# A routed two-FFN block on one core: the sync engine's list work moved two steps behind each list, and the closing sums shared by two engines

## The reference

```python
x = x + 0.5 * ffn(layernorm(x))     # 8 experts of width 256, the best 2 of them per token
x = x + attention(layernorm(x))     # 16 heads of 4, on the first 64 columns
x = x + 0.5 * ffn(layernorm(x))     # the same experts again

def ffn(xt):
    logits = xt @ gate_w.T + gate_b
    top_v, top_i = top_k(logits, 2)
    act = (xt @ w0.T + b0) * silu(xt @ w1.T + b1)          # per expert
    out_all = act @ w2.T + b2
    return sum over the 2 chosen of softmax(top_v) * out_all[chosen]
```

## Time and profile before

| | us |
|---|---|
| median of 3 runs | 752.5 (751.33 to 753.72) |
| the profiled execution, time | 752.53 |
| its span, first to last instruction | 750.8 |
| PE busy | 579.4 (77%) |
| DVE busy | 435.4 (58%) |
| POOL busy | 372.7 (50%) |
| ACT busy | 349.5 (47%) |

### The profile page before, as it was taken

One profiled execution on the slowest core, in us unless ns is written; L12 is line 12 of the kernel. 1 busy time (PEld: TensorE's weight loads), 2 busy tenths in 40 slices (PEclk: granted clock), 3 DMA queues, 4 the chain that ended last, 5 costly groups with the idle time before them and its releaser, 6 DMA issues. The chain is left out here.

```text
span 750.8 us, 14409 instructions
## 1 busy us (share of the span) xinstructions
PE 579.4 (77%) x4460; PEld 437.2 (58%) x4460; DVE 435.4 (58%) x1627; ACT 349.5 (47%) x806; POOL 372.7 (50%) x415
## 2 busy tenths in 40 slices
PE   3428995999971167988888888889898699699960
PEld 2317885889960023555555555556554489598950
DVE  6664461223332277678888888888863464244436
ACT  2004542455530002666666666666677356365530
POOL 4877750000007887445476767553422467566650
PEclk9999998999995555899999999999999799899985
DMA  8547653554611111111122222111100355555529
GB/s 281 166 124 248 192 188 119 195 163 149 198 43 39 51 55 49 50 49 49 49 63 63 63 63 62 56 50 49 59 21 16 118 168 189 173 171 170 172 66 332
DMA packets 65026, 86.01 MB, mean 115 GB/s; under 512 B 11096, under 2 KB 46648, under 8 KB 64152
## 3 DMA queue, kind: packets, MB, share of 16 engines
q1 hardware_dynamic: 52184, 63.29, 26.3%
q0 software_dynamic: 8640, 17.97, 7.8%
q10 hardware_dynamic: 4128, 3.83, 1.5%
HBM read 31.85 MB, written 30.56 MB: 83 GB/s over the span
## 5 line engine op out<-in xcount | busy, mean ns | idle before, releaser
L1164 DVE TENSOR_REDUCE attn_nm<-ps 128x2 f32<-128x512 f32 x256 | 168.9, 684 | 61.5 <-PE ps L883 59.8
L987 ACT ACTIVATE attn_pt<-ps 128x512 f32<-128x512 f32 x256 | 146.4, 594 | 74.4 <-PE ps L867 71.7
L671 DVE SCALAR_TENSOR_TENSOR experts_act<-ps,route_cols,experts_silu 128x256 f32<-128x256 f32 x170 | 81.4, 483 | 165.7 <-ACT experts_silu L635 165.5
L603 PE MATMUL ps<-experts_xT,experts_w 128*128 128x256 f32 x680 | 170.0, 394 | 0.0
L379 POOL DMA_INDIRECT x_rows<-route_xn,route_rows x128 | 125.3, 979 | 52.7 <-issue 34.8
L883 PE MATMUL ps<-attn_ka,attn_qa 128*128 128x256 bf16 x512 | 106.5, 295 | 47.7 <-DMA attn_qa<-kq_pieces 29.4
L603 PEld LDWEIGHTS ps<-experts_xT,experts_w 128*128 128x128 f32 x680 | 126.4, 196 | 15.0
L635 ACT ACTIVATE experts_silu<-ps,route_cols 128x256 f32<-128x256 f32 x170 | 80.2, 473 | 75.2 <-PE ps L603 74.7
L614 PE MATMUL ps<-w_table,experts_act 128*128 x680 | 101.5, 286 | 1.6 <-ACT experts_y_tokens L652 0.9
L867 PE MATMUL ps<-attn_qa,attn_ka 128*128 128x256 bf16 x512 | 99.3, 278 | 4.4 <-ACT attn_pt L987 2.4
L707 POOL DMA_INDIRECT y_tokens<-experts_y_tokens,experts_to x78 | 75.4, 966 | 43.4 <-ACT experts_y_tokens L652 28.5
(11 more groups left out here) (163 smaller groups left out, 712.9 us busy)
## 6 DMA issues: line engine op xcount, KB each, us to landing
experts_w<-w_table SPq DMA_DIRECT2D x85, 256.0 KB, 2.5
experts_x<-x_rows SPq DMA_DIRECT2D x85, 132.0 KB
y_rows<-experts_y_tokens SPq DMA_DIRECT2D x46, 128.0 KB, 1.9
x_rows<-no_rows SPq DMA_DIRECT2D x24, 132.0 KB
kq_pieces<-attn_kqp SPq DMA_DIRECT2D x16, 192.0 KB
x_rows<-route_xn,route_rows POOLq DMA_INDIRECT x128, 2.8
second_y<-y_tokens SPq DMA_DIRECT2D x8, 256.0 KB, 7.0
second_y<-y_tokens ACTq DMA_DIRECT2D x8, 256.0 KB, 7.4
```

What stands on the lines that cost most here:

```text
L603: mm = pe.matmul(ps[:, q % 2 * 2 + k, w * SLOTS:(w + 1) * SLOTS], m["w"][:, q % WR, at + k * P:at + (k + 1) * P], m["xT"][:, q % 2], start ...
L671: nc.vector.scalar_tensor_tensor(out=m["act"][:, q % 2, k], in0=ps[:, q % 2 * 2 + k, SLOTS:2 * SLOTS], scalar=route["col"](part, at, CH + ...
L987: nc.scalar.activation(pt[:, g % 2, j, :], ps[:, SBK[h % 2], :], ACT.Exp, scale=SCALE).then_inc(exp_done, 1)
L1164: nc.vector.tensor_reduce(nm[:, qc, 2 * pair:2 * pair + 2], ps[:, SA[k], :].rearrange("p (j t) -> p j t", t=S), AX.X, ALU.max, negate=True ...
```

## The change

SP's list work is split. `sp_list` keeps the blank rows, the wait for the list and the register loads; it is called two steps behind DVE's list, at step 13 for part 1 and at step 52 for part 3 (ahead of the loop for part 0, and where it was for part 2). A new `sp_rows`, at the part's first block, keeps the waits for sent rows and blank rows. At the end the sums are made 512 columns (two batches) at once: DVE takes six of the eight pairs, POOL takes pairs 2 and 5, and a semaphore counts each pair of loads.

```diff
     def sp_list(sp, part):
-        region = REGION_OF[part]
         if closed(part):
             for at in route["tails_of"](sp, part):
-                sp.dma_start(rows_of(x_rows[region % 2], at), const["no_rows"][:]).then_inc(tails, 16)
+                sp.dma_start(rows_of(x_rows[REGION_OF[part] % 2], at), const["no_rows"][:]).then_inc(tails, 16)
         sp.wait_ge(route["list_ready"], 3 * (part + 1))
         sp_starts(sp, first_block(part))
+
+    def sp_rows(sp, part):
         route["all_sent"](sp, part)
         if closed(part):
-            sp.wait_ge(tails, 16 * E * (region + 1))
+            sp.wait_ge(tails, 16 * E * (REGION_OF[part] + 1))
 
     def sp_x(sp, q):
         part, at = block_part(q)
-        if some(q)[1] and q not in start:
-            if at == 0:
-                sp_list(sp, part)
-            else:
-                sp_starts(sp, q)
+        if at == 0:
+            sp_rows(sp, part)
+        elif some(q)[1]:
+            sp_starts(sp, q)
...
-    def sp(sp, q, own):
+    def sp(sp, q, own, lists):
 
         if q - Y_LAG - 1 in own and q - Y_LAG - 1 < ONE:
             sp_y(sp, q - Y_LAG - 1)
+        for part, at in lists.items():
+            if q == at:
+                sp_list(sp, part)
...
+            blocks["sp_list"](sp, 0)
             for q in all_steps:
-                blocks["sp"](sp, q, own)
+                blocks["sp"](sp, q, own, {part: at + 2 for part, at in LISTS.items()})
...
-        def dve_take(dve, b):
-            dve.wait_ge(y_in[b // CHUNK], 16 * CHUNK)
-            tokens = xs[:, 2 * b:2 * b + 2, :]
-            nc.vector.tensor_tensor(tokens, tokens, y[:, b, :, 0, :], ALU.add).then_inc(half_done, 1)
-            dve.wait_ge(half_done, b + 1)
-            nc.vector.tensor_tensor(tokens, tokens, y[:, b, :, 1, :], ALU.add).then_inc(x_done, 1)
+        TAKERS = (0, 1, 3, 4, 6, 7), (2, 5)
+        def take(sync, eng, engine):
+            for n, i in enumerate(TAKERS[engine]):
+                sync.wait_ge(y_in[i], 32)
+                tokens, given = xs[:, 4 * i:4 * i + 4, :], y[:, 2 * i:2 * i + 2].rearrange("p b t r d -> p r (b t) d")
+                eng.tensor_tensor(tokens, tokens, given[:, 0], ALU.add).then_inc(half_done[engine], 1)
+                sync.wait_ge(half_done[engine], n + 1)
+                eng.tensor_tensor(tokens, tokens, given[:, 1], ALU.add).then_inc(x_done[engine], 1)
...
+            take(pool, nc.gpsimd, 1)
...
             for q in all_steps:
-                blocks["sp"](sp, q, own)
+                blocks["sp"](sp, q, own, {PARTS - 1: begin + TOP + 5})
```

More of the change, by code:

```diff
@@ L1662, in second_ffn @@
         y = late.enter_context(nc.sbuf_tensor("second_y", [P, NB, 2, 2, P], F32))
-        y_in = [c.enter_context(nc.semaphore(f"second_y_in{i}")) for i in range(4)]
-        half_done = c.enter_context(nc.semaphore("second_half_done"))
-        x_done = c.enter_context(nc.semaphore("second_x_done"))
+        y_in = [c.enter_context(nc.semaphore(f"second_y_in{i}")) for i in range(NB // 2)]
+        half_done, x_done = ([c.enter_context(nc.semaphore(f"second_{n}{i}")) for i in range(2)] for n in ("half_done", "x_done"))
         stored = c.enter_context(nc.semaphore("second_stored"))
@@ L1669, in second_ffn @@
         begin = own.start
-        CHUNK = NB // len(y_in)
+        TAKERS = (0, 1, 3, 4, 6, 7), (2, 5)
         block = late.enter_context(nc.Block())
-        def dve_take(dve, b):
-            dve.wait_ge(y_in[b // CHUNK], 16 * CHUNK)
-            tokens = xs[:, 2 * b:2 * b + 2, :]
-            nc.vector.tensor_tensor(tokens, tokens, y[:, b, :, 0, :], ALU.add).then_inc(half_done, 1)
-            dve.wait_ge(half_done, b + 1)
-            nc.vector.tensor_tensor(tokens, tokens, y[:, b, :, 1, :], ALU.add).then_inc(x_done, 1)
+        def take(sync, eng, engine):
[5 more added lines that the diff above has]
+                eng.tensor_tensor(tokens, tokens, given[:, 1], ALU.add).then_inc(x_done[engine], 1)
         def load(eng, b):
             rows = y_tokens[b * 2 * S:(b + 1) * 2 * S, :].rearrange("(p i) d -> p (i d)", i=4)
-            eng.dma_start(y[:, b].rearrange("p t r d -> p (t r d)"), rows).then_inc(y_in[b // CHUNK], 16)
+            eng.dma_start(y[:, b].rearrange("p t r d -> p (t r d)"), rows).then_inc(y_in[b // 2], 16)
         def store(eng, b):
-            eng.wait_ge(x_done, b + 1)
+            engine = 0 if b // 2 in TAKERS[0] else 1
+            eng.wait_ge(x_done[engine], TAKERS[engine].index(b // 2) + 1)
             eng.dma_start(out_dram[:, b], xs[:, 2 * b:2 * b + 2, :]).then_inc(stored, 16)
@@ L1748, in _ @@
                 blocks["dve"](dve, q, own, pick)
-            for b in range(NB):
-                dve_take(dve, b)
+            take(dve, nc.vector, 0)
         @block.sync
```

## The result

| | before | changed |
|---|---|---|
| median of 20 runs, us | 753.56 (750.33 to 754.89) | 749.73 (747.69 to 753.3) |
| ratio, 95% interval | | 0.9955 (0.9943 to 0.9968) |
| span of the profiled run, us | 750.8 | 747.6 |

The change makes the kernel faster by 0.45%, 3.4 us. The forecast was 7.2 us, and the measured 749.7 lies above its range of 742.7 to 748.8. Direction right, size more than twice too large.

A forecast was written before the change was run, and what follows sets the result against it. PE's pace was taken to bound the kernel, broken by SP's late row issues at blocks 19 and 63, with the end a separate stage. Terms -8.1 + 2.0 + 0.1 - 1.2 = -7.2 us gave 745.3 us, range 742.7 to 748.8.

The forecast's parts named there:

- That the stops are SP's own list work, and that moving it only moves them: PE's stops at blocks 19 and 63: SP's list work takes 9.4 to 10.4 us extra, moved but not removed.
- Part 1, 8.1 us gained: First FFN, list work at step 13: 10.4 lost today, less 1.6 at block 18 and 0.7 at block 19.
- The prediction's own sign of being wrong: It is wrong if SP's list work at the new places isn't 9.4 to 10.4 us long, among other signs.
- at its bare length: Block 18's stop was counted as 1.6 us of idle, with no slow products added behind it.
- rival (a): The clock falls at block 18's small stop too; slow products cost 2.5 us, giving 747.8 us; chance 0.11.
- The 0.7 for PE's own load: Block 19: PE's own load of ten experts, no longer covered by SP's lateness, loses 0.7 us (0.5 to 0.9).
- Part 3, 2.0 us lost: Second FFN, list work at step 52: 9.2 lost at block 57 plus 0.7 at block 63, against 7.9 today.
- The end, 1.2 us gained: Closing sums in pairs on DVE and POOL: the end becomes 1.2 us shorter (0.5 to 1.9).
- The additions no longer bound and the DMAs do: At the end, additions of 8.4 us on DVE and 4.2 on POOL fit within some 11 us of loads.
- The exclusion of DVE and POOL: At the end, if the two engines exclude each other, additions total 12.6 us; the earlier start alone brings about 1.
- The 0.1 for parts 0 and 2: Part 0 keeps its order; part 2's moved wait for sent rows costs 0 to 0.2 us, taken as 0.1 lost.

The follow-up runs named there:

- later: Against dve_all: list work one step later for part 1 (step 14) and two later for part 3 (step 54); 744.83 us, ratio 0.9903 to before.
- split: Against dve_all: list work cut into pieces that fit SP's idle time, nothing taken away; 735.49 us, ratio 0.9781 to before.
- dve_all: Against the changed kernel: DVE takes all eight pairs of closing sums and POOL none; 746.45 us, ratio 0.9915 to before.

## Why the prediction was wrong, point by point

**That the stops are SP's own list work, and that moving it only moves them: right.** It is 9.3 to 11.2 us long at six different steps (13, 14 and 16, 52, 54 and 58), and cutting it into pieces takes the 14.8 us lost at the two places down to 3.3 with all of it still done.

**Part 1, 8.1 us gained: too large by about 3, the first of the two steps that failed.** The stop came at block 18 as said. Two terms were mis-sized. The work took 10.3 to 11.2 us from the store to the rows where 9.6 were taken, and the rows' DMA 2.2 to 2.7 us to release PE where 2.1 were taken, so the rows were 2.7 to 3.2 us late and not 1.6. (The prediction's own sign of being wrong was list work that isn't 9.4 to 10.4 us long; in three of the five traces it was longer.) And the stop was counted "at its bare length": what rival (a) priced at 2.5 came, with 1.4 to 3.1 us of slower products, though behind a stop of 3 us and not of 1.6. Behind the stop of 2.5 in later it was 1.8, behind that of 1.1 in split 0.1, with a granted clock of 1.00; a stop of 1.6 stands in no run. The 0.7 for PE's own load, in turn, was covered. The loss is 4.4 to 6.2 in five traces, 5.4 in the mean, and 2.3 were forecast: a gain of 5.0 instead of 8.1.

**Part 3, 2.0 us lost: right.** The stop is 7.8 (7.2 said), the loss 9.4 to 11.1 over five traces, 10.3 in the mean, against 7.9 and 9.3 in the two with the old place, 8.6 in the mean: 1.7 lost.

**The end, 1.2 us gained: the wrong sign, the second step that failed.** "The additions no longer bound and the DMAs do" holds, as dve_all shows with exactly 1.2. What the sum left out is that POOL now has work near the end, and the barrier waits for POOL's drain, 7.7 us behind its last instruction. It was in the trace of before, covered:

```profile
L1661 POOLq DRAIN  x1: 10516/10516/10516, 726.3 to 726.3; - x1
```

It ended at 736.8 there, 7.8 us behind the last scatter (729.0), and the span went on for 14 us more. Making POOL busy later uncovered it. That is 2.9 us, and with the 1.2 gained a loss of 1.7. The exclusion of DVE and POOL, weighed in the prediction, is there too. It makes the last store leave later (16.8 us behind the first load's issue against 15.2 in dve_all), but SP sees the last store landed at about the same point, 19.0 and 18.8 us behind that issue, so it costs 0.2 at most.

**The sum.** -5.0 + 1.7 + 1.7 = -1.6 us by the terms as measured, where the runs give -3.4 (-4.3 to -2.4). For the moved list work alone it is -3.3 by the terms and -4.3 (-5.8 to -2.8) by the runs. So the terms explain both within some 1 to 2 us, and the cause of the remainder stays open: one profile of each kernel doesn't fix a mean of losses that vary by 2 us, and the untouched attention stage varies by more. The 0.1 for parts 0 and 2 is too small for any run here to show. The miss is 3.8 us; part 1's share of it is 3.1 and the end's 2.9, and the remainder, which no term explains, goes the other way and hides a part of both.

## What to carry to other kernels

Work on an in-order issuing queue isn't hidden by being moved earlier: list every place's room (issue time to need time, less the landing) and cut the work into pieces that fit it; here the pieces were worth some 15 us, where the move alone was worth 4.3. What the cut work hid then shows: here POOL's backlog. Before giving a free engine work near a barrier, look up how long its drain is there and when its last instruction would be. A stop of TensorE of 2.5 us or more cost here its length and 1.4 to 3.1 us of slower products behind it, so price it by measured stops and not by its length alone.

## What was not expected of the hardware

- GpSimd's drain at the closing barrier ended 7.7 to 7.8 us behind its last instruction in all nine traces, be it an indirect DMA (drain until 736.8, DMA instruction until 729.0, in before), an addition (747.4 and 739.7, changed) or a memset of one column (747.6 and 739.9).
- A DVE addition of 512 columns took 0.69 us alone and up to 1.6 or 1.7 us when one of POOL's ran; POOL's took 1.26 to 1.78. By the Trainium skill ("SBUF — State Buffer", "Who interferes with whom") the two exclude each other, and the trace agrees: in the changed kernel POOL's addition ran from 733.96 to 735.72, and DVE's, begun at 734.64, ended at 736.28 instead of about 735.33.
- Behind a stop of 2.5 to 3.2 us the granted clock was 0.57 to 0.75 over the 6 to 7 us that followed; in later it was still 1.00 during the stop of 2.5 itself (121.1 to 123.6) and 0.72 behind it.
- The longest of eight equal DMA issues on SP took 1.2 to 2.1 us in each of the five traces with the work at step 13, the median 0.33; at steps 14 and 16 none took over 0.36. What held it wasn't tried.
